# Attention on one core: value and sum matmuls of two key tiles in one burst, and a ring of six probability tiles

## What is computed

```python
qkv = x @ Wqkv.T
q, k, v = jnp.split(qkv, 3, axis=-1)          # heads: (2, 16, 2048, 32)
dots = jnp.einsum('bhid,bhjd->bhij', q, k) * dh ** (-0.5)
dots = jnp.where(causal_mask, -jnp.inf, dots)
attn = jax.nn.softmax(dots, axis=-1)
out = jnp.einsum('bhij,bhjd->bhid', attn, v)
return out @ Wout.T + bout
```

## Time and profile before

| | |
|---|---|
| median of 3 runs | 2804.41 us |
| profiled execution, span | 2807.5 us |
| self-attention, first to last of its matmuls | 274.76 to 1505.48 us |
| PE busy over the span | 2565.5 us, 91% |
| DVE busy | 1922.8 us, 68% |
| ACT busy | 1102.5 us, 39% |
| POOL busy | 782.2 us, 28% |

### The profile page before, as it was taken

The page is one execution under the profiler, slowest core; times in us unless marked ns, Lnnn a source line. Parts: engine busy times, 40 slices in busy tenths (PEclk is TensorE's granted clock), DMA queues, the critical chain, the costliest instruction groups (busy, mean ns, idle before and its releaser), DMA issues. The chain is left out here.

```text
span 2807.5 us, 45159 instructions
## 1 busy us (share of the span) xinstructions
PE 2565.5 (91%) x15124; PEld 1066.4 (38%) x15124; DVE 1922.8 (68%) x3126; ACT 1102.5 (39%) x2002; POOL 782.2 (28%) x275
## 2 busy tenths in 40 slices
PE   8998799998999899999996579999999999999998
PEld 3443233332323223233322335444444545454543
DVE  3333877877788687887863667776767676777765
ACT  3121255554555455555554434232332323232420
POOL 0001144454546163544445211111102021111100
PEclk9999899998999899999998889999999999999999
DMA  4343601102030202020002310101010100001000
GB/s 163 133 146 114 168 9 40 38 22 56 6 72 5 70 9 69 9 69 5 9 8 94 108 44 1 58 1 49 10 43 16 43 17 31 28 1 58 1 16 16
DMA packets 112453, 129.96 MB, mean 46 GB/s; under 512 B 8702, under 2 KB 87294, under 8 KB 112221
## 3 DMA queue, kind: packets, MB, share of 16 engines
q1 hardware_dynamic: 112221, 126.99, 15.1%
HBM read 83.18 MB, written 43.52 MB: 45 GB/s over the span
## 5 line engine op out<-in xcount | busy, mean ns | idle before, releaser
L553 ACT ACTIVATE probs<-st_ps 128x512 f32<-128x512 f32 (+3 forms) x1280 | 628.6, 533 | 597.3 <-PE st_ps L659 303.0
L584 DVE TENSOR_REDUCE seg_max<-s_ps 128x1 f32<-128x512 f32 (+3 forms) x1280 | 700.7, 600 | 232.4 <-PE s_ps L642 138.7
L642 PE MATMUL s_ps<-k_pair,q_pair 96*128 96x512 f16 (+3 forms) x1280 | 442.5, 368 | 69.7 <-DVE seg_max L584 57.2
L659 PE MATMUL st_ps<-q_pair,k_pair 98*128 98x512 f16 (+3 forms) x1280 | 438.6, 363 | 24.0 <-issue 17.8
L462 POOL TENSOR_TENSOR total<-total,probs 128x2048 f32<-128x2048 f32 x88 | 398.2, 4525 | 64.6 <-ACT probs L553 62.0
L679 PE MATMUL o_ps<-probs,v_sb 128*32 128x512 f32 (+3 forms) x2560 | 320.6, 574 | 0.0
L1360 PE MATMUL fps<-x2T,w_p_hi 128*128 128x512 f16 x1024 | 317.3, 379 | 0.0
L1360 PE MATMUL fps<-w_p_hi,hT 128*128 128x512 f16 x1024 | 304.8, 379 | 0.0
L659 PEld LDWEIGHTS st_ps<-q_pair,k_pair 98*128 98x128 f16 x1280 | 118.0, 98 | 375.1 <-ACT probs L553 286.8
L642 PEld LDWEIGHTS s_ps<-k_pair,q_pair 96*128 96x128 f16 x1280 | 126.8, 100 | 275.4 <-DVE seg_max L584 185.5
L462 POOL TENSOR_TENSOR total<-probs 128x2048 f32<-128x2048 f32 x24 | 108.8, 4532 | 356.6 <-ACT probs L553 356.6
(11 more groups left out here) (162 smaller groups left out, 3558.5 us busy)
## 6 DMA issues: line engine op xcount, KB each, us to landing
k_pair<-k_parts SPq DMA_DIRECT2D x96, 128.0 KB, 4.7
q_pair<-q_parts SPq DMA_DIRECT2D x96, 128.0 KB, 5.5
x_raw<-xT_in SPq DMA_DIRECT2D x8, 1024.0 KB, 5.8
q_parts<-qk_out SPq DMA_DIRECT2D x32, 256.0 KB, 2.5
k_parts<-qk_out SPq DMA_DIRECT2D x32, 256.0 KB, 2.5
v_rows<-v_out SPq DMA_DIRECT2D x32, 256.0 KB, 2.0
v_sb<-v_rows SPq DMA_DIRECT2D x8, 1024.0 KB, 10.8
o_parts<-o_out SPq DMA_DIRECT2D x32, 256.0 KB, 2.6
```

The source lines that it names most:

```text
L553: nc.scalar.activation(probs[:, k % NP, h, off:], st_ps[:, p % (2 * NVU) % RING, off:], ACT.Exp, scale=SCALE).then_inc(exp_done.sem, 1)
L584: nc.vector.reduce_max(seg_max[:, h, j, s:s + 1], s_ps[:, slot, 0:width], AX.X).then_inc(s_read.sem, 1)
L642: last = nc.tensor.matmul(s_ps[:, slot, 0:width], q_pair[a][0:NR, h, q0:q0 + P], k_pair[a][0:NR, h, s * CH:s * CH + width], start=True, st ...
L659: last = nc.tensor.matmul(st_ps[:, slot, off:], k_pair[a][:, h, kt * P:(kt + 1) * P], q_pair[a][:, h, c * CH + off:(c + 1) * CH], start=Tr ...
```

## The change

One lag, `BURST` = 4, takes the place of `VALUES` and `SUMS`. TensorE acts only for every second tile: with lag 4 of an odd tile k it issues values and sums of tile k - 1, then values and sums of tile k. The values of an even tile so come four steps later than before and its sums two steps later; the sums of an odd tile come two steps earlier. The number of tiles of a head group is even, and the last tile of every chunk is odd. All that hangs on `SUMS` moves two steps forward: ScalarE's copy of the denominators, the reciprocals (lags 7, 9, 11, 13), multiplication, output copy, remainder, store and SP's reload. The ring `probs` has six tiles in place of five (80 tiles are used per pass of the loop).

```diff
-    NP = 5
+    NP = 6
...
-    VALUES, SUMS = 4, 6
-    TAKEN = VALUES + 1, SUMS + 1
-    RECIPS = [SUMS + 3 + 2 * n for n in range(PIECES)]
+    BURST = 4
+    TAKEN = BURST + 1, BURST + 1
+    RECIPS = [BURST + 3 + 2 * n for n in range(PIECES)]
...
-                k = tile_at(s, SUMS, first, end)
+                k = tile_at(s, BURST, first, end)
...
-                k = tile_at(s, VALUES, first, end)
-                if k is not None:
-                    values(i, k)
-                k = tile_at(s, SUMS, first, end)
-                if k is not None:
-                    sums(i, k)
+                k = tile_at(s, BURST, first, end)
+                if k is not None and k % 2 == 1:
+                    for n in (k - 1, k):
+                        values(i, n)
+                        sums(i, n)
```

## The result

The changed kernel takes 2929.73 us (median of 4 runs, 2927.29 to 2932.17) against 2802.93 us of the kernel before (4 runs): a ratio of 1.0452, 95% interval 1.0438 to 1.0466. It is 4.5% slower. The forecast was 2819, its range ended at 2885.

A forecast was written before the change was run, and what follows sets the result against it. Two engines taking turns bound the self-attention: TensorE on the diagonal, VectorE in the openings of chunks 1 to 3. Per head group -3.7 + 2.8 + 0.7 + 0.9 + 1.0 = +1.7 us, times eight +14: 2819 us, range 2750 to 2885.

The forecast's parts named there:

- Step 1: TensorE's switches between scores and value or sum groups: 43 fewer at 0.22 us, 9.5 us per head group, 76 over eight.
- Step 2: VectorE's idle time behind each burst: 1.0 us for two value groups, 1.9 with a sum, diagonal 2.3 and 1.5.
- Step 3: Later of two engines per stretch, per head group: diagonal 3.7 us gained, openings of chunks 1 to 3 2.8 lost, middles 0.7 lost.
- The diagonal's -3.7: Four stretches over a chunk's diagonal tiles: 1.3 + 1.3 + 0.5 + 0.6 = 3.7 us gained per head group.
- step 5: The rest, at nothing: ring of six (0 to -9 us), ScalarE's two copies in a row, SP's reload, TensorE's wait before `total`.
- the +43: Whole kernel by the interleaving rule alone: the sum without the diagonal's gain of 3.7, about +43 us.
- Step 4: VectorE's f16 output copy beside POOL's addition: longer wait 0.9 us, burst held until it is through +1, per head group.
- The clock term: Burst behind the output copy at the lower clock: at most +1.4 us, three times; taken as +1 per head group.
- B: Rival: VectorE starves behind every burst and the clock drops, +8 us per head group, 2868 us; chance 0.18.
- its own condition: The starvation rival decides where VectorE's busy time plus 30 us per head group exceeds 146.9; the prediction had 117.8 + 30.
- C: Rival: output copy starts before POOL's addition, takes 0.42 us instead of 3.5, 77 us less on VectorE, about 2745; chance 0.06.
- A: Rival: TensorE is the bound almost everywhere, fewer switches give a quarter to all of 76 us, 2728 to 2785; chance 0.24.

The follow-up runs named there:

- copy_back: Changed kernel with multiplication, output copy, remainder and store two steps later, reciprocals left early: 2780.75 us, 0.9918 of the kernel before.
- addition_after_copy_burst: Changed kernel with POOL's additions, except that of a chunk's second tile, one step later, behind the remainder: 2778.45 us, 0.9912 of the kernel before.
- addition_after_copy_before: Kernel before with POOL's additions, except that of a chunk's second tile, three steps later, behind the remainder: 2753.18 us, ratio 0.9822.

## Why the prediction was wrong, step by step

*What bounds the kernel* was read rightly: two engines in turns, openings held by VectorE, TensorE ahead elsewhere.

*Step 1, fewer switches, 9.5 us per head group of TensorE's time.* The price of TensorE's time is right (a joined group 0.86 to 0.88 us), its worth to the kernel is not: 23 or 24 of the 43 switches removed gave 0 net (1.0003 and 1.0000).

*Step 2, idle time behind bursts.* Right in kind, 20% short: 2.34, 2.91 and 1.80 for 1.9, 2.3 and 1.5 us.

*Step 3, stretch by stretch, failed too.* The diagonal's -3.7 did not come. In its first stretch the sum has VectorE's 8.01 us alone, without the idle time behind the two bursts of chunk 0; by step 2 these are 2.3 and 0.6, which with 8.01 make 10.9 against 10.55, no gain but a loss. Measured, VectorE idles 3.5 us there (12.45 less 8.97) and the stretch, 10.42 before, takes 12.45. The later of two engines was taken from busy plus idle time of VectorE alone; ScalarE starves as well (3.54 us), and its two copies, put at nothing in step 5, stand ahead of the exponentials. Diagonal and middles together were to give -3.0 per head group and gave +3.9: 7 us, 55 over eight. The rule of the Trainium skill that the prediction weighed (Perfetto Trace Analysis, section Optimization Strategy: interleave the regimes) fits better than I let it. With the copy out of the way, undoing the interleaving costs 41 to 49 us with the copy on ScalarE and 25 with the addition moved. The runs agree with the rule's sign; the +43 was my own sum, and comes near.

*Step 4 is the one that failed most.* "The output copy" was the right place and both of its effects were named: the copy would ask sooner after the addition's start and wait up to its whole length, and the burst that stood beside it would now wait until it is through. I priced the first at 0.3 us (measured: median +0.6, sum 8 us, as priced), and the second only as clock, +1 per head group. With step 3's +2.8, the openings were to cost 4.7 us per head group; they cost 12.6. What I left out is the burst's own time. Before, a value group (1.0 us) ran inside the copy for nothing (the text says a sum and a value group, but the sum group stood ahead of the copy, at 1136.96); after, 2.7 us of burst come behind the copy in series, 4.6 at half clock, and VectorE idles for nearly all of it (4.2 to 4.4 us), three times per head group. The clock term was too small as well: the row with 1.62 us was only partly at the lower level, a group wholly at it takes 1.94, and the burst became 1.9 us longer, not 1.4. `copy_back` takes away 149 us and `addition_after_copy_burst` 151, more than the whole loss; but the kernel before gains without the stall too. Against it under the same edit, the step's part of the 127 us is 78 (copy on ScalarE) or 102 (addition moved), where the forecast had 1.9 per head group, 15 us. The other 49 or 25 are what bursts cost by themselves, where steps 1 to 3 add up to -0.2 per head group, nothing.

*Step 5:* the ring of six at nothing, right (0.9999). The early tail without the stall, ScalarE's two copies in it, costs 8 us (2772 and 2764).

*The rivals.* B names the mechanism (VectorE restarts behind a burst at half clock; the clock in the openings falls clearly under 0.93, and did, to 0.77 to 0.85; TensorE's idle time there was to double, and did, from 7.1 to 14.3 us), but spread over all bursts and at +8 per head group. By its own condition it held already: 117.8 + 30 is 147.8, above the 146.9. C is false: the copy did not get ahead of the addition (0.29 us behind it). The Trainium skill's rule quoted there (SBUF — State Buffer, section SBUF: two separate sides: an exclusive lock, for the whole instruction of whoever starts first) holds in every row of the copy: 0.42 us with the addition elsewhere, up to 4.7 beside it, ending with it. The page limits it, on VectorE's side, to instructions in a two-port performance mode or with two SBUF inputs; the trace agrees in so far as not all are held: a reciprocal inside an addition (1212.92, in the addition at 1209.97) takes its 0.94 us as elsewhere. A is false: fewer switches gained nothing in any run.

*What stays open:* how the 25 to 49 us of bursts without the stall divide between VectorE and ScalarE, and over the stretches, and what the shifted additions cost in `addition_after_copy_before`.

## What to carry to other kernels

When an instruction that will be held up moves in a queue, price it by what the other engines can still do while it is held: ask which work of theirs stands ahead of their next wait on it, and which falls behind. Work that left that shadow was paid here in full, and at the lower clock that came with the longer stall. Time saved on TensorE, which feeds two engines through rings of three, was worth nothing here, since the saving came as longer absences. And when an edit removes a loss, apply it to the kernel before too: 151 us gained on the one side were 102 of the difference, since the other side gained 50.

## What the runs showed of the hardware

- A VectorE copy of 128x512 from f32 to f16 takes 0.42 us, and beside a POOL addition of 4.5 us it ends 0.3 us after that addition, whatever its start: 2.76, 3.51, 4.00 and 4.50 us for starts 2.07, 1.28, 0.82 and 0.29 us into it. The same copy on ScalarE takes 0.63 us beside the addition, and a VectorE reciprocal of 128x128 0.94 us inside one as outside.
- After TensorE had stood 4.41 us its matmuls ran at the lower level at once (0.63 us for a score of 0.39, 1.94 for a group of 1.04); after 2.27 us the first scores still took 0.39 and the later ones and one group ran slow (0.63 and 1.62); after 1.34 us none did in the place shown, but behind the same stall of 1.34 us in an earlier head group of that run, at 686.53, scores took 0.63 from 2 us on. With 3.64 us of zero matmuls in the longer stall a group took 1.06 behind it, and over the kernel that was worth 55 us.
